# First layer's plain scores: the causal bias moves from a matmul on TensorE into VectorE's pass for the row maximum

## What is computed

```python
# first block
scores = jnp.einsum('bhqd,bhkd->bhqk', q, k) * scale
scores = jnp.where(causal, scores, -jnp.inf)
attn = jax.nn.softmax(scores, axis=-1)
out = jnp.einsum('bhqk,bhkd->bhqd', attn, v)
x = x + gt_a * (out @ Wproj + bproj)
x = x + gt_m * (gelu(xm @ W1 + b1) @ W2 + b2)
# second block: the same shape, without the causal mask and the gates
```

## Time and profile before

| What | Value |
|---|---|
| Median of 3 runs | 1178.01 us (1175.23 to 1180.79) |
| Profiled execution, its own time | 1178.39 us |
| Its span in the trace | 1176.2 us |
| Mean granted clock of TensorE | 0.971 |
| First layer's attention, about | 17 to 385 us |
| Second layer's attention, about | 600 to 960 us |
| DMA, mean over the span | 69 GB/s |

### The profile page before, as it was taken

How to read it: one execution, slowest core, us unless ns; L and a number is a source line. 1 busy time by engine, 2 the same in 40 slices (tenths; PEclk the granted TensorE clock), 3 DMA queues, 4 the chain that set the end, 5 groups by cost and what they waited for, 6 DMA issues and landing times.

```text
span 1176.2 us, 24117 instructions
## 1 busy us (share of the span) xinstructions
PE 1091.0 (93%) x9228; PEld 958.2 (81%) x9228; DVE 752.3 (64%) x1627; ACT 622.6 (53%) x1255; POOL 252.9 (22%) x252
## 2 busy tenths in 40 slices
PE   3989999999999788999985899999999987999998
PEld 3778989998987577899874788888888766988997
DVE  5456666666665457765645687878787646566653
ACT  1146666666665643443331677777777666334431
POOL 5101221211211244223321112121212013121111
PEclk9789999999999999999987899999999999999999
DMA  7547767567561010000057473746456400000001
GB/s 214 114 70 118 129 114 119 97 110 124 135 101 23 7 55 10 13 10 11 14 85 159 72 96 64 97 65 96 70 91 77 58 2 1 19 33 22 19 19 36
DMA packets 50826, 81.49 MB, mean 69 GB/s; under 512 B 8916, under 2 KB 23476, under 8 KB 49620
## 3 DMA queue, kind: packets, MB, share of 16 engines
q1 hardware_dynamic: 49752, 78.37, 37.5%
q10 hardware_dynamic: 960, 1.57, 1.2%
HBM read 22.64 MB, written 8.44 MB: 26 GB/s over the span
## 4 chain that ended last, share of the span: by engine, by line
PE 83%; DVE 4%; DMA 4%; SPq 3%; ACT 2%; issue 2%; POOL 2%; ACTq 1%; POOLq 0%; DVEq 0%
PE g_bank L541 14%; PE st_bank L541 13%; PE o_bank L629 9%; PE o_bank L541 8%; PE s_bank L541 7%; PE s_bank L596 6%; PE st_bank L615 5%; PE s_bank L590 3%; PE st_bank L609 3%; PE st_bank L611 3%; PE s_bank L592 2%; PE g_bank L687 2%; SPq L406 2%; DMA k_stack<-qk_split 2%; DMA q_stack<-negmaxT 1%
## 5 line engine op out<-in xcount | busy, mean ns | idle before, releaser
L807 ACT ACTIVATE probs<-st_bank 128x384 f32<-128x384 f32 (+1 forms) x512 | 273.6, 548 | 156.5 <-PE st_bank L611 89.9
L910 ACT ACTIVATE probs<-st_bank,cols 128x512 f32<-128x512 f32 x128 | 88.0, 689 | 217.6 <-PE st_bank L541 191.1
L541 PE MATMUL st_bank<-qk_split,q_stack 128*128 128x512 f32 x768 | 187.3, 402 | 15.4 <-ACT probs L910 10.8
L1099 DVE TENSOR_REDUCE maxima<-s_bank 128x2 f32<-128x512 f32 x256 | 168.9, 685 | 42.5 <-PE s_bank L596 41.6
L541 PEld LDWEIGHTS st_bank<-qk_split,q_stack 128*128 128x128 f32 x768 | 144.8, 191 | 53.0 <-ACT probs L910 13.8
L1095 DVE TENSOR_REDUCE maxima<-s_bank 128x3 f32<-128x384 f32 x256 | 138.7, 554 | 60.1 <-PE s_bank L592 56.9
L596 PE MATMUL s_bank<-k_stack,q_stack 97*128 97x256 f32 x512 | 115.9, 309 | 17.8 <-DMA k_stack<-mask_dram 10.6
L541 PE MATMUL g_bank<-xmT,wa 128*128 128x256 f32 x768 | 122.7, 299 | 4.8 <-POOL xmT L1271 4.8
L629 PE MATMUL o_bank<-probs,v_sb 128*32 128x256 f32 (+1 forms) x2048 | 124.7, 361 | 1.6 <-ACT probs L807 1.6
L596 PEld LDWEIGHTS s_bank<-k_stack,q_stack 97*128 97x128 f32 x512 | 80.1, 195 | 44.4 <-issue 28.0
L1271 POOL TENSOR_TENSOR xmT<-xm_full,xmT 128x512 fp32r<-128x512 f32 x32 | 42.3, 1322 | 331.8 <-ACT xmT L873 331.8
(11 more groups left out here) (114 smaller groups left out, 2104.7 us busy)
## 6 DMA issues: line engine op xcount, KB each, us to landing
q_stack<-qk_split SPq DMA_DIRECT2D x192, 128.0 KB, 4.5
k_stack<-qk_split SPq DMA_DIRECT2D x180, 128.0 KB, 6.0
gate_rows<-gate_dram SPq DMA_DIRECT2D x32, 128.0 KB, 3.4
w_dram<-w_in SPq DMA_DIRECT2D x8, 512.0 KB, 7.2
wm_f32r<-w_dram SPq DMA_DIRECT2D x4, 1024.0 KB, 7.9
out<-x_sb SPq DMA_DIRECT2D x8, 512.0 KB, 2.9
x_sb<-x_in SPq DMA_DIRECT2D x4, 512.0 KB, 7.8
k_stack<-qk_split ACTq DMA_DIRECT2D x12, 128.0 KB, 8.7
```

Source lines behind the costliest of these rows:

```text
L541: last = mm(dst, weights[i], rows[j], start=(f == 0 and n == 0), stop=(f == tiles - 1 and n == len(TERMS) - 1))
L807: activation(probs[:, h % 8, 0:n], st_bank[h % 2][:, 0:n], ACT.Exp, scale=SCALE)\
L910: activation(h_full[:, m % 2], st_bank[m % 2][:, :], ACT.Gelu, bias=cols[:, cb + m:cb + m + 1])\
L1099: v.reduce_max(maxima[:, gb.mod(2), 0:2, slot], bank[:].rearrange("p (i n) -> p i n", n=T), AX.X).then_inc(max_done, 1)
```

## The change

The third matmul of `scores` goes. In its place VectorE makes two passes for a head, one for each half of the queries, with tensor_tensor_reduce: it adds a bias to the scores in the PSUM bank, writes the sum back there, and takes the maximum of the row in the same pass. For the first half of the queries (128 columns) the bias is the triangle; for the second (256 columns) it is 128 zeros with the triangle behind them. For that the triangle lies in fp32 in the second half of tri_wide, and GpSimd writes zeros to the first. There are two maxima for a head, so the joining of the second and third goes. In the first layer the wait for s_ready stands apart from the instruction behind it (`wait_apart`: the wait, then an increment of a semaphore that nobody waits for). `LAG` and the slots are not changed; the transposed scores keep their bf16 bias matmul. The scratch for dynamic DMA goes from 4096 to 1024 bytes.

```diff
+LOWEST = -3.0e38
+        tri_wide = sb("tri_wide", [P, T])
-        maxima = sb("maxima", [P, 2, 3, H])
+        maxima = sb("maxima", [P, 2, NT, H])
-        tri = in_probs(P)
+        tri = tri_wide[:, P:T]
...
                     mm(bank[:, P:3 * P], q[:, P:T], k, start=True, stop=False)
-                    mm(bank[:, 0:P], q[:, 0:P], k[:, 0:P], start=False, stop=False)
-                    last = mm(diagonal(bank), ident16[:], tri16[:].unsqueeze(1).to_broadcast((P, 2, P)),
-                              start=False, stop=True)
+                    last = mm(bank[:, 0:P], q[:, 0:P], k[:, 0:P], start=False, stop=True)
...
-                        dve.wait_ge(s_ready, gb.count(H, s + 1))
+                        if layer == 0:
+                            wait_apart(dve, s_ready, gb.count(H, s + 1), dve_passed)
+                        else:
+                            dve.wait_ge(s_ready, gb.count(H, s + 1))
...
                         if layer == 0:
-                            v.reduce_max(maxima[:, gb.mod(2), 0:3, slot],
-                                         bank[:, 0:3 * P].rearrange("p (i n) -> p i n", n=P), AX.X)\
-                                .then_inc(max_done, 1)
+                            for i in range(NT):
+                                keys = slice(i * P, (2 * i + 1) * P)
+                                last = v.tensor_tensor_reduce(
+                                    out=bank[:, keys], in0=bank[:, keys], in1=tri_wide[:, T - (i + 1) * P:T],
+                                    scale=1.0, scalar=LOWEST, op0=ALU.add, op1=ALU.max,
+                                    accum_out=maxima[:, gb.mod(2), i, slot:slot + 1])
+                            last.then_inc(max_done, 1)
...
-                if layer == 0:
-                    v.tensor_tensor(m[:, 1], m[:, 1], m[:, 2], ALU.max).then_inc(max_joined, 1)
-                    dve.wait_ge(max_joined, g.count(1, 1))
...
             set_up_first()
+            dve.wait_ge(power_set, 2)
...
+            g_.memset(tri_wide[:, 0:P], 0.0).then_inc(power_set, 1)
             g_.memset(half_power[:], -0.5).then_inc(power_set, 1)
...
-            pool.wait_ge(power_set, 1)
+            pool.wait_ge(power_set, 2)
...
-    nc = bacc.Bacc("TRN2", target_bir_lowering=False, num_devices=1, dynamic_dma_scratch_size=4096)
+    nc = bacc.Bacc("TRN2", target_bir_lowering=False, num_devices=1, dynamic_dma_scratch_size=1024)
```

More of the change, by code:

```diff
@@ L268, in build @@
         max_done = sem("max_done")
-        max_joined = sem("max_joined")
         negmax_hi = sem("negmax_hi")
@@ L1094, in step @@
                         if layer == 0:
-                            v.reduce_max(maxima[:, gb.mod(2), 0:3, slot],
-                                         bank[:, 0:3 * P].rearrange("p (i n) -> p i n", n=P), AX.X)\
-                                .then_inc(max_done, 1)
+                            for i in range(NT):
[5 more added lines that the diff above has]
+                            last.then_inc(max_done, 1)
                         else:
-                            v.reduce_max(maxima[:, gb.mod(2), 0:2, slot],
+                            v.reduce_max(maxima[:, gb.mod(2), :, slot],
                                          bank[:].rearrange("p (i n) -> p i n", n=T), AX.X).then_inc(max_done, 1)
@@ L1147, in negative_maximum @@
                 dve.wait_ge(max_done, g.count(H, H))
-                if layer == 0:
-                    v.tensor_tensor(m[:, 1], m[:, 1], m[:, 2], ALU.max).then_inc(max_joined, 1)
-                    dve.wait_ge(max_joined, g.count(1, 1))
                 wait(dve, negmaxT_ready, g.count(1, -1))
-                v.tensor_scalar(dst[:, :, 0], m[:, 0:NT], -1.0, None, ALU.mult).then_inc(negmax_hi, 1)
+                v.tensor_scalar(dst[:, :, 0], m, -1.0, None, ALU.mult).then_inc(negmax_hi, 1)
                 dve.wait_ge(negmax_hi, g.count(1, 1))
-                v.scalar_tensor_tensor(out=dst[:, :, 1], in0=m[:, 0:NT], scalar=-1.0, in1=dst[:, :, 0],
+                v.scalar_tensor_tensor(out=dst[:, :, 1], in0=m, scalar=-1.0, in1=dst[:, :, 0],
                                        op0=ALU.mult, op1=ALU.subtract).then_inc(negmax_ready, 1)
```

## The result

Five runs of the changed kernel have a median of 1164.34 us (1161.70 to 1168.54); five of the kernel before, on the same chip, 1176.63 us. The ratio is 0.9896, with a 95% interval of 0.9866 to 0.9926: 12.3 us less (8.7 to 15.8 by the interval), where 14 were forecast. The profiled execution took 1161.7 us, with a span of 1159.9 us; it is the fastest of the five, so 12.3 and not its own 16.7 is the gain to be explained. Lines have moved: L590 and L591, the plain scores, are L591 and L592 now; L609 to L611, the transposed ones, are L608 to L610; the passes for the maximum are L1099.

What follows compares the result with a forecast made beforehand. TensorE, busy throughout a full step, was taken as the bound. 17.9 us saved less 0.7, 1.1, 0.8 and 0.7 gave 14.6, rounded to 14, off about 1178: 1164 us, range 1149 to 1192.

Steps and rivals of the forecast that it cites:

- Part 1: TensorE's plain scores: 256 bias matmuls go, each head saves 0.07 us, 17.9 us in all.
- rival 1: TensorE's plain scores: L591 keeps 0.06 us, a head saves the full 0.13, about 1151 us; chance 0.10.
- Part 2: VectorE's maxima: 256 reductions become 512 tensor_tensor_reduce, 0.78 us a pair, hidden under TensorE with 1.5 us a step to spare.
- Rival 3: VectorE's passes: the maximum's write is a second instruction waiting for an empty pipe; slower, 1206 us or more; chance 0.18.
- Its threshold: VectorE in a full step: the pair may cost 0.87 us before VectorE sets the period.
- Part 3: Four slots from plain to transposed scores: the room of 0.26 us for negmaxT's transfers shrinks by 0.21.
- the 0.5 us charged: Distance to the transposed scores: 0.5 us in all for steps whose transfer takes longer.
- Part 4: First two steps with scores: VectorE bounds the first, k_stack comes 0.8 us later, the second's saving goes into a wait.
- charges of 1.1, 0.8 and 0.7: First steps: 1.1 us not saved in the first, 0.8 for later k_stack, 0.7 lost in the second's wait.
- the 0.2 charged: Distance to the transposed scores: 0.2 us for the last step of scores.

Runs made afterwards that it cites:

- e1: Changed kernel with the bias matmul of the plain scores put back, VectorE's new passes kept: 1179.95 us, ratio 1.0012.
- e2: Kernel before with the plain scores' bias matmul taken out, old reduction kept, first layer's exponent scaled by 0.001: 1165.26 us, ratio 0.9907.
- e3: Changed kernel with the 128-column matmul of the plain scores made 256 columns wide: 1162.87 us, ratio 0.9877.
- e9: Changed kernel with one more unused VectorE maximum over 128 elements for each first-layer head: 1163.17 us, ratio 0.9870.
- e4: Changed kernel with one more unused VectorE maximum over 256 elements for each first-layer head: 1177.62 us, ratio 0.9982.
- e5: Changed kernel with LAG 3 instead of 4, transposed scores three slots behind the plain ones: 1286.62 us, ratio 1.0925.
- e6: Changed kernel with LAG 5 instead of 4, transposed scores five slots behind the plain ones: 1187.22 us, ratio 1.0075.
- e11_sums_in_sbuf: Changed kernel with the sums of tensor_tensor_reduce written to SBUF instead of back to PSUM: 1162.59 us, ratio 0.9860.
- e12_plain_wait: Changed kernel with the plain wait on s_ready, without the semaphore increment behind it: 1162.71 us, ratio 0.9877.

## Why the prediction was right, step by step

**Part 1, TensorE.** The forecast of 0.07 us for a head was met by 0.074, for the reason given: e1 and e2 tie the gain to this matmul, e3 shows that fp32 loads and not streaming set the pace around it. One thing was wrong in it: I said that L591's piece of the chain would grow from 0.06 to 0.11 or 0.12, and that 0.06 would mean rival 1. It stayed at 0.06, and the load's cost stood on the row behind, 0.12 to 0.17. By my own sign I would have called rival 1 true and been off by a factor of two. 256 x 0.074 would be 18.9 us in all, against 17.9; 176 heads of it are the eleven full steps.

**Part 2, VectorE.** Hidden, as said; the pair was mis-sized, 0.63 in place of 0.78. The durations came out near their rows (306 and 466 ns against 295 and 426, the difference being the write into PSUM), and the write of the maximum is indeed an instruction of its own. What I left out in my value, though rows 8 showed it for reductions, is the overlap: every pass starts about 0.08 us before the last one's end, and the write of the maximum lies beside the next pass. So VectorE is at 16.62 us a step, a little under the 17 to 18 named. The Trainium skill, page "VectorE: DVE Perf Modes", section "Two Vector instructions with no wait between them", counts a written accumulator as two instructions; the 349 rows of 143 ns agree. What its section "The DRAIN you can't avoid" says of the next instruction starting on an empty pipe the timeline doesn't show: 0.47 us passes, the next one 0.38 behind. The same section adds what the prediction left out, that an instruction that isn't held starts earlier, and with that the timeline agrees. (The advice on fewer instructions, which the prediction puts under this section, stands in the same page of the Trainium skill, section "Rules for kernel authors".) Rival 3 took a second instruction and an empty pipe together, and fell with the empty pipe. Its threshold was right: e9 below it, e4 above.

**Part 3, the distance.** In full steps TensorE waits for negmaxT once at four slots, for 0.4 us, so the 0.5 us charged was about right. That four has little room is shown by e5. The prediction looked at one side only; e6 shows the other.

**Part 4, the edges.** The first step with scores is 13.7 us long (some 14 said), from the start of VectorE's first pass at 45.58 to the end of its last at 59.30, and TensorE waits 3.96 us behind it for k_stack, against 3.30 in the earlier trace rows (a difference of 0.7, with 0.8 charged). Windows of the third and fourth stretch between marks, before and then after, have the rest:

```profile
55.36:75.88 20.52, 16.73 (x136) 15.57 (x135) 13.24 (x30) 8.35 (x17) 2.16 (x3) 0.83 0.62 105
75.88:98.15 22.27, 20.21 (x216) 17.99 (x215) 13.63 (x31) 13.32 (x30) 2.16 (x3) 1.00 0.66 94
```

```profile
55.49:76.58 21.09, 15.70 (x120) 14.53 (x120) 14.42 (x79) 8.23 (x17) 2.16 (x3) 0.76 0.65 97
76.58:97.99 21.41, 19.01 (x201) 16.79 (x200) 15.88 (x80) 13.17 (x30) 2.15 (x3) 1.00 0.66 94
```

The stretch with the longer wait has a granted clock of 0.76 in place of 0.83 and is 0.6 us longer; the next gains 0.9. By the pace the 45 heads up to the fifth mark would save 3.3 us; 0.2 are left. The prediction's charges of 1.1, 0.8 and 0.7 would have left 0.6.

**The last steps** are the term that the profiled execution doesn't bear out. Two steps' saving, some 2.3 us with the 0.2 charged, should have come between the marks at 320.93 and 582.60; this stretch is 0.9 longer. The timeline of the kernel after has this line in the last step with scores:

```profile
350.83 0.58 PE L608 MATMUL st_bank<-q_stack,k_stack 99*128 99x256 f32 x1 [1.87 <-DMA q_stack<-negmaxT]
```

The wait itself is 0.3 us more than before's 1.53 at the same place. But behind it TensorE runs ten microseconds at a granted clock of 0.51 (its lower level, the third window above), where before's same stretch has 0.83. Ten microseconds at 0.51 in place of 0.83 do 3.2 us less work at full clock. Three runs with the same matmuls as after tell the saving and the clock apart. Their ten microseconds behind this wait (e9_dve_128, e11_sums_in_sbuf, e12_plain_wait), and last before's:

```profile
353.20:363.20 10.00, 10.00 (x92) 8.36 (x92) 7.35 (x40) 5.51 (x12) 0.00 (x0) 0.83 0.04 10
352.32:362.32 10.00, 10.00 (x92) 8.40 (x92) 5.77 (x33) 5.47 (x12) 0.00 (x0) 0.83 0.04 12
349.91:359.91 10.00, 10.00 (x77) 8.50 (x77) 5.52 (x27) 3.90 (x9) 0.00 (x0) 0.66 0.04 10
365.19:375.19 10.00, 10.00 (x94) 8.58 (x94) 5.09 (x11) 4.91 (x11) 0.00 (x0) 0.83 0.03 10
```

| Run | Clock behind the wait | Sixteenth mark to the first transposes of the MLP, us |
|---|---|---|
| before | 0.83 | 69.0 |
| e9_dve_128, e11_sums_in_sbuf | 0.83 | 67.1, 66.3 |
| e12_plain_wait | 0.66 | 67.9 |
| after | 0.51 | 69.9 |
| e2_pe_alone, e3_wide | 1.00 | 64.8, 65.5 |

At before's own 0.83 the stretch is 2.0 and 2.7 us shorter: the 2.3 us of the last steps are there, and in after's profiled execution the clock took them. The prediction had no term for it. What sets the clock there isn't shown. Kernels with the same matmuls and nearly the same wait had 0.51, 0.66, 0.83 and 1.00, and e1_both, which has before's matmuls and the new passes, had 1.00, so nothing here says that the change lowers it.

**Luck in the number.** The 1164 was met to 0.3 us, but before's median was 1176.63 us here and not the 1178.01 of the forecast, and the sum of 14.6 had been rounded down to 14. What the runs bear out is 12.9 us in full steps, a little at the first ones, and some 2 us in the last ones that the clock can take. The forecast's terms add up to about as much, so it was right in its mechanism and in its size; that it agrees to a few tenths is luck, with an interval of 8.7 to 15.8 us for the gain.

## What to carry to other kernels

Price a removed matmul by the pace of the chain with it and without it, and ask what its neighbours then expose: behind a 128-column matmul the next fp32 load stands open, so 0.13 us in the trace was worth 0.074. On VectorE count the distance from start to start, not the rows: 1.06 us of rows were 0.63 us of time, and a threshold worked out from one step (0.87 us here) tells better than a share of busy time whether an engine has room. Before a pipeline's distance is changed, list every transfer that its ends release, on both sides.

## What the runs showed of the hardware

- A 128-column fp32 matmul ahead of an fp32 load leaves its cost on the matmul behind (0.17 in place of 0.12 us); widening it to 256 columns costs 0.009 us for a head.
- tensor_tensor_reduce takes 306 ns for 128x128 and 466 for 128x256 in place in PSUM, 289 and 420 into SBUF. The instruction that writes its maximum takes 143 and 83 ns, beside the next pass; passes start 0.08 to 0.09 us before the last one's end.
- Behind a wait of 1.5 to 1.9 us at the same place, ten microseconds of TensorE had a granted clock of 0.51, 0.66, 0.83 or 1.00 in kernels whose matmuls are alike there. From 1.00 to 0.51 the stretch grew from 65.5 to 69.9 us: more than the wait.
